# A DLRM tower with a two-thread CIN: the order of the first stagings and block loads, and the distance between the threads

## The reference, cut to what matters

```python
e = jnp.stack([tbl_f[ids[:, f]] for f in range(32)], axis=1)   # (1024, 32, 16)
x0 = xk = e
outs = []
for W in (W0, W1, W2):                                         # (32, hk_1, 64)
    xk = relu(einsum('bmd,bhd,mhk->bkd', x0, xk, W))
    outs.append(sum(xk, axis=2))                               # over d
z = concatenate(outs, axis=1)                                  # (1024, 192)
h = concatenate([z, dense_ctx], axis=1)                        # (1024, 208)
h = maximum(h @ W_top1 + b_top1, 0)                            # 512 wide
h = maximum(h @ W_top2 + b_top2, 0)                            # 256 wide
y = h @ W_top3
```

## Time and profile before

| | us |
|---|---|
| median of 3 runs (623.82 to 624.78) | 623.99 |
| the profiled execution, its own time | 625.95 |
| its span | 624.0 |
| TensorE busy | 600.8 (96%) |
| VectorE busy | 515.1 (83%) |
| GpSimd busy | 444.2 (71%) |
| ScalarE busy | 322.4 (52%) |
| DMA queues of SyncE, share of 16 engines | 62.8% |

### The profile page before, as it was taken

One profiled execution on the slowest core, in us unless ns is written; L12 is line 12 of the kernel. 1 busy time (PEld: TensorE's weight loads), 2 busy tenths in 40 slices (PEclk: granted clock), 3 DMA queues, 4 the chain that ended last, 5 costly groups with the idle time before them and its releaser, 6 DMA issues.

```text
span 624.0 us, 8470 instructions
## 1 busy us (share of the span) xinstructions
PE 600.8 (96%) x2926; PEld 211.4 (34%) x2926; DVE 515.1 (83%) x454; ACT 322.4 (52%) x545; POOL 444.2 (71%) x346
## 2 busy tenths in 40 slices
PE   4779899999999999999999999999999999999998
PEld 3532333333333333333333333333333333333454
DVE  0258698999989998999899998999899999888500
ACT  1333565555565454565545554545565456643564
POOL 6778858788787878787887878786878875556300
PEclk9999999999999999999999999999999999999999
DMA  4597787867887777677767887777667868750000
GB/s 128 184 333 257 283 308 292 285 239 258 274 283 274 258 244 253 222 289 246 258 227 282 283 275 245 252 283 253 222 236 265 289 242 273 269 197 0 1 1 0
DMA packets 45199, 144.49 MB, mean 232 GB/s; under 512 B 9619, under 2 KB 24085, under 8 KB 32870
## 3 DMA queue, kind: packets, MB, share of 16 engines
q1 hardware_dynamic: 36966, 141.85, 62.8%
q0 software_dynamic: 8192, 2.11, 4.0%
HBM read 139.21 MB, written 4.72 MB: 231 GB/s over the span
## 4 chain that ended last, share of the span: by engine, by line
PE 87%; POOL 5%; DMA 5%; issue 2%; SPq 1%; ACT 0%
PE acc L677 77%; POOL gathered L506 5%; PE x_ps L672 5%; DMA x_rows<-gathered 3%; PE sums_ps L746 2%; PE x_ps L746 2%; DMA gathered<-in_table,idx 1%; SPq L419 0%; DMA x_wide<-x_rows 0%; SPq L408 0%; DMA base_sb<-in_base 0%; PE sums_ps L672 0%; POOL idx L529 0%; ACT x_wide L593 0%; ACT x_wide L596 0%
## 5 line engine op out<-in xcount | busy, mean ns | idle before, releaser
L627 DVE TENSOR_TENSOR dve_ring<-x_wide,x_ps 128x1024 f32<-128x1024 f32 x428 | 489.2, 1215 | 62.2 <-issue 47.2
L677 PE MATMUL acc<-dve_ring,w_sb 128*64 128x512 f32 (+1 forms) x1744 | 474.6, 589 | 6.8 <-DVE dve_ring L627 6.8
L506 POOL DMA_INDIRECT gathered<-in_table,idx x256 | 243.8, 952 | 69.7 <-issue 64.1
L518 POOL TENSOR_TENSOR pool_ring<-x_wide,x_sb 128x1024 f32<-128x1024 f32 x84 | 199.3, 2383 | 76.7 <-ACT x_sb L577 46.9
L677 PEld LDWEIGHTS acc<-dve_ring,w_sb 128*64 128x64 f32 x1744 | 150.9, 138 | 293.4 <-issue 268.6
L677 PE MATMUL acc<-pool_ring,w_sb 128*64 128x512 f32 x336 | 131.6, 592 | 0.0
L567 ACT ACTIVATE x_ps<-acc 64x512 f32<-64x512 f32 (+1 forms) x132 | 73.5, 557 | 110.5 <-PE acc L677 108.2
L677 PE MATMUL acc<-pair_squares,w_sb 128*64 128x512 f32 (+1 forms) x264 | 113.9, 581 | 1.2 <-ACT pair_squares L547 1.2
L577 ACT COPY x_sb<-layer_out 64x512 f32<-64x512 f32 x128 | 79.0, 617 | 3.6
L547 ACT ACTIVATE pair_squares<-x_ps 128x1024 f32<-128x1024 f32 x32 | 32.8, 1025 | 88.5 <-PE sums_ps L672 88.2
L572 ACT ACTIVATE layer_out<-acc 64x512 f32<-64x512 f32 (+1 forms) x98 | 56.8, 579 | 2.4 <-PE acc L677 1.0
(11 more groups left out here) (36 smaller groups left out, 127.1 us busy)
## 6 DMA issues: line engine op xcount, KB each, us to landing
x_wide<-x_rows SPq DMA_DIRECT2D x96, 1024.0 KB, 8.0
x_wide<-x_rows SPq DMA_DIRECT2D x32, 768.0 KB, 5.6
x_wide<-x_rows SPq DMA_DIRECT2D x32, 256.0 KB
gathered<-in_table,idx POOLq DMA_INDIRECT x256, 4.5
x_rows<-gathered SPq DMA_DIRECT2D x32, 128.0 KB
w_sb<-in_w SPq DMA_DIRECT2D x2, 512.0 KB, 5.7
x_rows<-gathered SPq DMA_DIRECT2D x32, 16.0 KB
x_wide<-in_W_top SPq DMA_DIRECT2D x1, 512.0 KB, 4.3
```

What stands on the lines that cost most here:

```text
L506: pool.indirect_dma_start(gathered[:, c, j % 2, e * DIM:(e + 1) * DIM], None, table, bass.IndirectOffsetOnAxis(ap=idx[:, unit, e:e + 1], a ...
L518: nc.gpsimd.tensor_tensor(pool_ring[:, c], x0_step(c, j, layer, 2 * d, 2).rearrange("p (s n) -> p s n", n=COLS), x_sb[:, layer - 1, c, :]. ...
L627: nc.vector.tensor_tensor(dve_ring[:, c, slot:slot + width, :], x0_step(c, j, layer, i, width).rearrange("p (s n) -> p s n", n=COLS), x_ps ...
L677: done = nc.tensor.matmul(part, w, x[:, cols], start=first, stop=last)
```

## The change

Three things are changed. `DELTA` goes from 18 to 20, and with it all slots of thread 1 and of the split unit (0,0). `sum_slot` puts the sums of (0,2) 10 slots into unit (0,1), not 4. In SyncE's hand-written list block 2 of (0,0) is issued before the staging of (1,0); the stagings of (0,1) and (1,1) are awaited before block loads that stood between, and blocks 0 and 1 of (0,1) come behind the staging of (1,1). No DMA, matmul or product is added or removed.

```diff
-DELTA = 18
+DELTA = 20
...
-    return begin(c, j) + (4 if j > 0 else (20, 10)[c])
+    if j == 0:
+        return begin(c, 0) + (20, 10)[c]
+    return begin(c, j) + (10 if (c, j) == (0, 1) else 4)
...
             load_block(0, 0, 1)
+            load_block(0, 0, 2)
             stage(1, 0)
-            load_block(0, 0, 2)
             sp.wait_ge(x0_staged[1], 32)
             load_first_step(1, 0)
             load_block(0, 0, 3)
             load_block(1, 0, 0)
             load_block(1, 0, 1)
             stage(0, 1)
-            load_block(1, 0, 2)
             sp.wait_ge(x0_staged[0], 64)
             load_first_step(0, 1)
+            load_block(1, 0, 2)
             load_block(1, 0, 3)
-            load_block(0, 1, 0)
-            load_block(0, 1, 1)
             stage(1, 1)
             sp.wait_ge(x0_staged[1], 64)
             load_first_step(1, 1)
+            load_block(0, 1, 0)
+            load_block(0, 1, 1)
             load_block(1, 1, 0)
             load_block(1, 1, 1)
```

## The result

The changed kernel takes **626.89 us** (median of 20 runs, 624.45 to 628.96) against 624.6 us for the kernel before, measured beside it (20 runs, 622.47 to 627.47). The ratio is 1.0036, 95% interval 1.0022 to 1.0050: by it 2.25 us slower, where 1.3 us faster was forecast, and outside the range of 621.0 to 625.4. The traced run has a span of 626.5 us, its own time is 628.25.

The account below looks back on a forecast made before the run. TensorE, full from about 80 us, was held at the start by waits through DMA. Sums of (1,2) at 92.4 against 93.72, all else nothing: 1.3 us off the median 623.99, 622.7 us, range 621.0 to 625.4.

Parts of the forecast that it names:

- The baseline: Whole time: the 1.3 us gain read from the profiled run was taken off the median 623.99, giving 622.7 us.
- the DMA chain: Stagings up to (1,2): its first step lands at 92.4 and sets the sums of (1,2), 1.3 us earlier than 93.72.
- TensorE's order: Start, thread 1: two idle slots go, sums of (1,2) at 91.5 by TensorE and VectorE alone, 2.2 us earlier.
- Nothing for the steady rounds and the tail: After the sums of (1,2): later rounds and the tail were costed at no change.
- Rival 4: Steady rounds: distance 20 bunches VectorE's products, TensorE waits 0.2 us in each of 14 rounds, 2.8 us, 625.5; chance 0.07.
- Block 2 and the gathers: Staging of (1,0): gathers slowed by block 2 of (0,0), so issued at 29.6, between 28.05 and 30.06.
- rival 1: Staging of (1,0): gathers don't mind block 2, it lands at 30.5, time 621.1; chance 0.22.
- Its landing, 2.45 us later: Staging of (1,0): lands 2.45 us after issue, at 32.05 against 31.60, so block 3 is 0.45 us late.
- piece (e): DMA: the 4 MB group behind the staging of (0,2), up to the landing of the staging of (1,2), takes 14.8 us.
- Rival 3: Stagings queue up: gathers at worst, (0,1) and (1,1) land 1.9 behind the last load; 625.9 us; chance 0.11.
- The clock, costed at nothing: TensorE before 28.30 to about 31 us: the 1.2 GHz level stays and costs nothing; without cover half of 4.93 us.

Follow-up runs that it names:

- e1_order: Kernel before with the change's DELTA 20 and later sums of (0,2), keeping SyncE's old list; 624.39 us, 1.0005.
- e3_block2: Kernel before with one edit: block 2 of (0,0) issued ahead of the staging of (1,0); 625.64 us, 1.0027.
- e4_rest: Kernel before with all the change's edits of SyncE's list except the move of block 2 of (0,0); 628.15 us, 1.0069.
- e11_cover_delta: e7_cover with DELTA 20 instead of 18, sums of (0,2) in their old slot; 623.71 us, 0.9999 of the kernel before.
- e2b_sp: Second trace of the kernel before with the change's SyncE list, DELTA 18 and old slots; this run 628.29 us, that kernel's median 628.85 us, 1.0090.
- e7_cover: Kernel before; blocks 0, 1 of (0,1) queued between staging of (1,1) and its wait, block 3 of (0,1), (1,1) behind later stagings; 623.09 us, 0.9980.
- e10_delta: Kernel before with DELTA 20 instead of 18 and nothing else; 627.62 us, 1.0055.

## Why the prediction was wrong

- **The baseline: failed.** The sum subtracted 93.72 - 92.4 = 1.3 us from the median, though the run it was read from had been 1.96 us over that median. The prediction wrote this number down and didn't ask where the 2 us were. Own time less span is 1.95, 1.92 and 1.75 us in the traces of before, the second of before and the change, so the 2 us lay inside the span: in the 2.27 us of DMA waits, of which the second trace has 0.79, and in a start 0.8 us later (50.38 against 49.56). Against the second trace the 92.4 us forecast for the sums of (1,2) is 1 us later than 91.36, not 1.3 us earlier than 93.72. A run at the median would, by an estimate from these traces (623.99 - 1.93 - 530.26), start them at 91.8: against that, 92.4 is 0.6 us slower. This step alone turns the sign. The rest of the miss is the DMA chain below: for the changed kernel the same estimate (626.89 - 1.8 - 530.63) gives 94.5, which is 2.1 us later than the 92.4 forecast.
- **TensorE's order: the placing held, its worth didn't.** Placed: 51.2, 61.0, 78.3, 91.5, which is 41.1 us of path, with waits of 0.9 and 0.6 for VectorE (the second did not come). Measured 41.75 in e1_order, piece by piece 0.97, 9.81, 17.47 and 13.50 us where 0.8, 9.8, 17.3 and 13.2 stood. But "by TensorE and VectorE alone worth 2.2 us" compared it with a path of 43.34 that held the 2.27 us of DMA waits. The fair comparison is 40.94, and the order is 0.8 us longer.
- **Nothing for the steady rounds and the tail: a little off.** VectorE made TensorE wait nowhere after the sums of (1,2); the tail is 530.6 against 530.25 us. Rival 4 (2.8 us) didn't come.
- **Block 2 and the gathers: right.** The staging of (1,0) was to be issued at 29.6. In the six traces with block 2 ahead it goes out at 28.88 to 29.93, mean 29.27; in twelve with the old place at 26.90 to 28.41, mean 27.74. So the gathers do lose 1.5 us to one megabyte of loads, and rival 1 falls. By the Trainium skill, "DMA: Bandwidth & Descriptors", section "Queues, rings and completion order", an engine alternates between its queue rows packet by packet, so gathers needn't wait for a load queue to empty; the traces show that sharing still slows them.
- **Its landing, 2.45 us later: too short.** In the three traces of the change it took 4.08, 2.61 and 3.22 us, and landed at 33.05, 32.54 and 32.41, against 32.05 forecast and 31.60 before. The 31.60 was late as well: the twelve traces with the old place have it at 28.97 to 32.24, mean 30.9, the six with the new one 32.6. So block 2 ahead of it costs this landing 1.7 us, where 0.45 was forecast.
- **The DMA chain: right in kind, short in size.** Staging of (0,1) forecast 44.1, measured 45.53, 45.71, 44.37; (1,1) 53.6, measured 57.01, 56.12, 54.86; (0,2) 74.7, measured 76.74, 76.63, 74.78; (1,2) 89.5, measured 92.91, 92.40, 90.03. The mis-sized terms are 12.0 us up to the staging of (0,1), which took 12.0 to 13.2, 9.5 us from (0,1) to (1,1), which took 10.4 to 11.5, and piece (e), 14.8 us from the earlier trace rows, which took 15.3 to 16.2. The 21.1 us between them took 19.7 to 20.5. The prediction said that a bare staging leaves the engines empty, and its sum has no term for it. Rival 3's mechanism came about in part: it named a staging of (1,1) after 54.9 as the turning point, and forecast 625.9 with 0.11.
- **Where the 2.25 us are.** The means of the table's traces: start 51.85 against 49.97 (+1.9), path without waits 41.8 against 41.0 (+0.8), DMA waits 1.06 against 1.53 (-0.5), tail +0.4; sum +2.6. The start is the weakest of them: in all twelve traces with the old place of block 2 the first matmul of (1,0) L1 stands between 49.56 and 53.99, mean 51.5, and in the six with the new one between 50.42 and 53.09, mean 51.8. The start has two parts. The first is when VectorE begins the last two products of (0,0) L1, which the prediction put down to the landing of block 3: 37.64 to 40.65, mean 39.2, with the old place, 38.50 to 41.17, mean 39.7, with the new one. The second is the 11.9 us from there to the first matmul of (1,0) L1, the same in eleven of the eighteen traces; the clock, below, lengthens it. That block 2 costs time is shown by e3_block2's runs (1.7 us). e3's own trace is late just there, with the products at 41.17, but over the six traces these products come only 0.5 us later than over the twelve. So where the usual run loses the 1.7 us stays open.
- **The clock, costed at nothing: right in two traces of three.** The prediction costed the 1.2 GHz level at 29 to 31 us at nothing. In the first trace of the change it isn't there, the 28 matmuls take 3.96 us instead of 4.93, and nothing is gained, since the sums of (1,0) then wait 3.04 us for DMA instead of 1.49. But each of the three traces has a fall at 36 to 45 us, which the prediction didn't have, and in the second it meets a stretch where VectorE waits for TensorE. Timeline of VectorE in the first, timelines of VectorE and TensorE in the second:

```profile
39.75 2.35 DVE L629 TENSOR_TENSOR dve_ring<-x_wide,x_ps 128x1024 f32<-128x1024 f32 x2 [5.27 <-issue]
44.86 3.48 DVE L629 TENSOR_TENSOR dve_ring<-x_wide,x_ps 128x1024 f32<-128x1024 f32 x3 [2.75 <-issue]
```

```profile
40.00 2.35 DVE L629 TENSOR_TENSOR dve_ring<-x_wide,x_ps 128x1024 f32<-128x1024 f32 x2 [6.11 <-issue]
46.07 3.48 DVE L629 TENSOR_TENSOR dve_ring<-x_wide,x_ps 128x1024 f32<-128x1024 f32 x3 [3.72 <-issue]
```

```profile
41.27 3.20 PE L679 MATMUL acc<-dve_ring,w_sb 128*64 128x256 f32 x16 [2.26 <-DVE dve_ring L629]
```

The 16 matmuls take 3.20 us instead of 2.21 in the trace of before, VectorE stands idle 3.72 us instead of 2.75, and the first matmul of (1,0) L1 comes 12.89 us after the products, not 11.94: the fall cost 1 us. e4_rest (13.21) and e11_cover_delta (13.34) have the same fall at the same place. With the list of the change but without its late sums (e2b_sp) a fall came at 79, where it costs too.

## What to carry to other kernels

Before a gain is counted, ask whether the waits that it removes are in the median run: compare the traced run's own time with the median, and where they differ by as much as the gain, take a second trace. A write that must land before the next read can go is worth covering with loads queued between it and its wait (e7_cover, 0.9980; with the change's numbers the same cover gave nothing, 1.0010). Moved bare to an earlier place, the staging of (1,1) landed at 54.9 to 57.0 us against 56.8 and 58.8, and the one behind it, of (0,2), at 74.8 to 76.7 against 71.9 and 74.1. An order with more slack, here distance 20 together with the later sums, was worth something only as insurance: it brought the new list from 1.0090 to 1.0036, and with the old list it gave nothing (1.0005). Distance 20 without the later sums cost 0.0055.

## What was not expected of the hardware

The start varies by several microseconds where little or nothing was changed: the first matmul of (1,0) L1 stands at 50.96 to 52.89 us in three traces of the changed kernel, and at 49.56 to 53.99 in the twelve with the old place of block 2, while the tail of distance 18 lies between 530.23 and 530.33 us in all its traces. The spread of times, 622.3 to 627.9 us for the kernel before, is thus made ahead of the sums of (1,2). In the traces it comes from when the stagings and block 3 land (3.5 us between the earliest and the latest start of the last products of (0,0) L1), from waits for DMA (none to 2.8 us) and from the clock.

A fall of TensorE's clock to the 1.2 GHz level lasted 3 to 4 us in most places (1.65 us lost in e2b_sp) and 6 to 7 us in e10_delta (3.1 us lost). It came after waits of TensorE, but not after each and not by length: 2.00 us brought one and 2.77 us none at the same place. Its cost goes by what waits for TensorE's matmuls then: 3.1 us in e10_delta, 1.65 in e2b_sp, 1 us in the second trace of the change. The one at 29 to 31 us in the trace of before cost nothing: the first trace of the change is without it and gained nothing by that.
